# First projections of a cross-attention kernel in another order, and the FFN weights made in later slots

## The reference, cut to what matters

```python
x = x + xattn(layernorm(x), ctx, ctx, mask, w_q, w_k, w_v, w_o)
# xattn: 16 heads of 64; q, k, v projections;
#   softmax(where(mask, -inf, q k^T / 8)) v, heads joined, @ w_o
x = x + ffn(layernorm(x), kernel, bias, a, b)
# ffn: w = quantize_int4(kernel); y = x w + bias + (x a) b
```

## Time and profile before

| what | value |
| --- | --- |
| three executions | 502.39, 502.15, 498.56 us |
| profiled execution: span from first to last instruction | 499.3 us |
| its own time | not given apart from the span |
| mean granted TensorE clock | 0.979 of full speed |
| busy: PE, DVE, ACT, POOL | 451.8, 406.2, 327.6, 398.7 us |
| chain of waits: PE, DVE, ACT, POOL | 43%, 27%, 16%, 8% of the span |
| busy PE, first and second 20 us | 10.76 and 15.70 us |

### The profile page before, as it was taken

The page is one execution under the profiler, slowest core; times in us unless marked ns, Lnnn a source line. Parts: engine busy times, 40 slices in busy tenths (PEclk is TensorE's granted clock), DMA queues, the critical chain, the costliest instruction groups (busy, mean ns, idle before and its releaser), DMA issues.

```text
span 499.3 us, 15466 instructions
## 1 busy us (share of the span) xinstructions
PE 451.8 (90%) x5855; PEld 328.7 (66%) x5855; DVE 406.2 (81%) x1110; ACT 327.6 (66%) x845; POOL 398.7 (80%) x659
## 2 busy tenths in 40 slices
PE   3968989999999999999999999999999999888874
PEld 1434756777766866777766866687667867576662
DVE  4986779987988989788988989898988888778662
ACT  5967566875677766776677766776667666656530
POOL 5687478999788977788788978798797977889931
PEclk9999799999999999999999999999999999899897
DMA  8602685798957996689857985798677877669950
GB/s 284 213 23 43 125 178 113 137 182 169 168 115 144 196 144 118 123 185 161 145 116 141 195 158 119 144 182 160 129 141 128 158 143 142 126 126 177 155 127 27
DMA packets 218817, 71.91 MB, mean 144 GB/s; under 512 B 202785, under 2 KB 216882, under 8 KB 218738
## 3 DMA queue, kind: packets, MB, share of 16 engines
q1 hardware_dynamic: 217680, 69.25, 71.4%
q0 software_dynamic: 480, 1.31, 0.9%
q10 hardware_dynamic: 578, 0.30, 0.2%
HBM read 14.71 MB, written 4.19 MB: 38 GB/s over the span
## 4 chain that ended last, share of the span: by engine, by line
PE 43%; DVE 27%; ACT 16%; POOL 8%; issue 4%; DMA 2%; SPq 0%; DVEq 0%; POOLq 0%; ACTq 0%
PE ps_b L915 32%; ACT arena L673 8%; DVE ps_a L803 7%; PE ps_a L983 6%; DVE arena L796 4%; DVE arena L785 2%; ACT arena L652 2%; DVE arena L871 2%; DMA arena<-in_L_xattn_w_q_dram 2%; POOL arena L580 2%; PE ps_b L1035 2%; POOL arena L584 2%; PE ps_b L1004 2%; ACT arena L664 1%; DVE arena L807 1%
## 5 line engine op out<-in xcount | busy, mean ns | idle before, releaser
L915 PE MATMUL ps_b<-arena 128*128 128x65 f16 (+3 forms) x3348 | 323.6, 249 | 6.1 <-DVE arena L871 3.4
L915 PEld LDWEIGHTS ps_b<-arena 128*128 128x128 f16 x3348 | 224.5, 99 | 81.8 <-issue 6.1
L673 ACT ACTIVATE arena<-ps_a,arena 128x160 f32<-128x160 f32 x512 | 160.0, 396 | 92.6 <-DVE arena L807 84.0
L584 POOL TENSOR_TENSOR arena<-arena 128x512 f16<-128x512 f32 x128 | 148.6, 1161 | 0.0
L580 POOL CAST arena<-arena 128x512 f16<-128x512 f32 x128 | 78.4, 613 | 54.4 <-ACT arena L673 53.1
L803 DVE TENSOR_REDUCE ps_a<-ps_a 128x4 f32<-128x640 f32 x128 | 105.3, 822 | 0.0
L983 PE MATMUL ps_a<-arena 64*128 64x160 f16 x1536 | 76.2, 232 | 13.2 <-ACT arena L673 13.2
L983 PEld LDWEIGHTS ps_a<-arena 64*128 64x128 f16 x1536 | 50.8, 95 | 38.2 <-issue 20.9
L1004 PE MATMUL ps_b<-arena 128*128 128x65 f16 x512 | 72.1, 194 | 0.0
L871 DVE TENSOR_TENSOR arena<-ps_b,arena 128x256 f32<-128x256 f32 x128 | 54.3, 424 | 4.4
L796 DVE TENSOR_TENSOR arena<-ps_b,arena 128x512 f16<-128x512 f32 x60 | 41.1, 686 | 19.1 <-ACT arena L664 17.8
(11 more groups left out here) (139 smaller groups left out, 424.3 us busy)
## 6 DMA issues: line engine op xcount, KB each, us to landing
arena<-in_x_dram SPq DMA_DIRECT2D x8, 512.0 KB, 5.5
mask_u<-in_x_dram SPq DMA_DIRECT2D x32, 128.0 KB, 3.0
out_dram<-mask_u SPq DMA_DIRECT2D x32, 128.0 KB, 2.6
arena<-arena SPq DMA_TRANSPOSE x128, 4.0
arena<-arena SPq DMA_DIRECT2D x24, 65.0 KB, 2.7
arena<-in_L_xattn_w_q_dram SPq DMA_DIRECT2D x1, 1024.0 KB, 8.7
arena<-in_L_xattn_w_k_dram SPq DMA_DIRECT2D x1, 1024.0 KB, 10.7
arena<-in_L_xattn_w_v_dram SPq DMA_DIRECT2D x1, 1024.0 KB, 12.2
```

The source lines that it names most:

```text
L584: nc.gpsimd.tensor_tensor(lo_main, main, hi_main, ALU.subtract)
L673: ins = nc.scalar.activation(probs[k % 2][:, h, :], p_scores[k % 2][:, h % 2, h // 2 * WINDOW:(h // 2 + 1) * WINDOW], ACT.Exp, bias=neg_ma ...
L915: mm = nc.tensor.matmul(dst, a, c, start=(first and at == 0), stop=(last and at == n - 1))
```

## The change

Three things. The first projections get another order: `k0` directly behind `c`, and `r0`, `r1` ahead of `v0`, `v1`; the scores of units 0 to 3 lie behind `q6`, `q7`, `k3` and `v0` (a table, `SCORES_BEHIND`), not behind `k1`, `k2`, `v0` and `r0`. The statistics for the second input lie behind `q7` and `k2`, and POOL's power is taken in slot 0. In the slots of the first batch, the keys of the second batch come in slots 1 and 2, its input's transposes in slot 3, and the queries and values behind them in other slots than before. The FFN pieces move from slots 1, 3, 5 to 6, 8, 10 on DVE, and from 4 to 9 on ACT. For that, the LoRA product gets memory of its own.

```diff
@@ -375,15 +373,17 @@
-        FIRST_PROJ = [["c", "x0"], ["x1"], ["k0", "k1"], ["k2"],
-                      ["k3", "q0"], ["q1"], ["q2"], ["q3", "q4"],
-                      ["q5"], [], ["q6"], ["q7", "v0"],
-                      ["v1"], [], [], []]
+        FIRST_PROJ = [["c"], ["k0", "k1"], ["k2", "k3"], ["x0", "x1"],
+                      ["q0"], ["q1"], ["q2"], ["q3"],
+                      ["q4", "q5"], [], ["q6"], ["q7"],
+                      ["v0"], ["v1"], [], []]
...
-        ALL_PROJ = AHEAD + ["h", "c", "q6", "k0", "q7", "k1", "k2", "k3", "v0", "v1", "r0", "r1"]
+        ALL_PROJ = AHEAD + ["h", "c", "k0", "q6", "k1", "q7", "k2", "k3", "r0", "r1", "v0", "v1"]
+        SCORES_BEHIND = {"q6": 0, "q7": 1, "k3": 2, "v0": 3}
+        NORM_SLOT = 0
@@ -589,11 +594,12 @@
             split_low(nc.gpsimd, 3)
-            norm(2)
 
             def slot(s):
                 if s.k < LAST - 1:
                     split_probs(s.k)
+                if s.k == NORM_SLOT:
+                    norm(2)
@@ -705,11 +711,14 @@
-                if name in ("v1", "r1"):
-                    half = int(name == "r1")
-                    for t in range(ST // 2 * half, ST // 2 * (half + 1)):
+                if name == "r1":
+                    exps(2)
+                if name == "v1":
+                    for t in range(ST // 2):
                         norm_apply(t, 2)
-                    exps(2 + half)
+                    exps(3)
+                    for t in range(ST // 2, ST):
+                        norm_apply(t, 2)
@@ -719,7 +728,7 @@
-                if s.k == 4:
+                if s.k == 9:
                     act.wait_ge(ffn_made, 1)
@@ -810,18 +819,12 @@
-                if name == "k1":
-                    maxima(0)
-                if name == "k2":
-                    maxima(1)
-                if name == "v0":
-                    maxima(2)
-                if name == "r0":
-                    maxima(3)
-                if name == "c":
+                if name in SCORES_BEHIND:
+                    maxima(SCORES_BEHIND[name])
+                if name == "q7":
                     for t in range(ST):
                         norm_stats(t, 32)
-                if name == "k0":
+                if name == "k2":
                     norm_var()
@@ -880,11 +883,11 @@
-                if s.k == 1:
+                if s.k == 6:
                     ffn_grid(dve)
-                if s.k == 3:
+                if s.k == 8:
                     ffn_weights(dve)
-                if s.k == 5:
+                if s.k == 10:
                     dve.wait_ge(split_hi, 5)
...
@@ -1058,6 +1055,8 @@
                 for i, name in enumerate(s.proj):
+                    if s.k < NS and name in ("k0", "q0"):
+                        pe.wait_ge(item_done, first_item("c" if name == "k0" else "x1"))
                     item(s, i, name)
```

## The result

| | us, median (lowest to highest) | ratio to before, 95% interval |
| --- | --- | --- |
| before | 501.79 (498.56 to 502.39, 4 runs) | |
| after | 515.64 (511.94 to 515.9, 4 runs) | 1.0282 [1.0238, 1.0325] |
| forecast | 511.8 (503.5 to 517.5) | |

What follows compares the result with a forecast made beforehand. In slots with a projection, a 3.43 us ACT-DVE round trip sets the pace. Terms 3.5 + 1.4 + 3.2 - 1.1 = 7.0, with the clock's 2.6 9.6, on 502.15 give 511.8 us (chance 0.50); range 503.5 to 517.5.

Steps and rivals of the forecast that it cites:

- A: Program start up to the second batch's k0: scores(2) at 44.5, k0 at 55.8 to 55.9 against 52.41, +3.5 us.
- B: Second batch's k0 to maxima(4): DVE does three keys' low parts first, 4.4 us against 2.97, +1.4 us.
- C: Slots 4 to 15: round-trip loop, q0 behind x1's low part, moved FFN pieces, q5, v1 in slot 13; +3.2 us.
- D: POOL at unit 16: it was behind by about 1.7 us and swallows two thirds of that delay, -1.1 us.
- order, sum: Terms A to D over the first batch and start, without the clock: 3.5 + 1.4 + 3.2 - 1.1 = 7.0 us.
- clock: Half clock behind the 4.7 us wait ahead of the second batch's k0, over three keys and scores: +2.6 us.
- walk: Step-by-step timing from the first projections: scores(2) at 44.5, c's copy at 54.6, second batch's k0 at 55.8 to 55.9.
- rival with both stretches: Rival: the wait ahead of scores(2) also brings half clock, doubling r0, r1, v0, +3.9 us: 515.7; chance 0.14.
- No second stretch: Rival: no second half-clock stretch, so the order's 7.0 us alone: 509.2; chance 0.18.
- given back: Rival: DVE's added work in slots 6 to 15 hides, POOL bounding that batch's end: +2.5 us, 504.7; chance 0.11.
- Faster: Rival: keys run straight behind c, if ACT copies c before 48 us: -5.2 us, 496.9; chance 0.07.
- POOL's root: POOL's normalization root behind the first splitting of probabilities holds the second some 2 us; claimed to cost nothing.

Runs made afterwards that it cites:

- experiment with all waits filled: After, with filler matmuls in four waits of PE (first k0, scores(2), second batch's k0, its q0): 507.14 us, ratio to before 1.012.
- experiments 4: Before, with only the new slot table of the first batch: 507.1 us, ratio 1.0109.
- 7: After, with the old start (first projections, scores 0 to 3, statistics and normalizations as before): 505.33 us, ratio 1.007.
- 10: Before, with 36 filler matmuls in PE's wait ahead of x0 in slot 0: 499.52 us, ratio 0.9975.
- 12: Kernel 11 with filler also at the program's start, 50 matmuls during the mask load and 14 ahead of the first query: 499.89 us, ratio 0.9989.
- experiments 5: Before, with only the FFN pieces moved to slots 6, 8, 10 and 9: 501.45 us, ratio 1.0004.
- 11: The fastest kernel: before with filler ahead of x0 and the FFN grid on DVE moved from slot 1 to slot 0: 498.62 us, ratio 0.995.

## Why the prediction was right, and where not

**The forecast.** Slower, inside the range, by the mechanism named; 3.8 under the median. The experiment with all waits filled takes most of the clock out, so its trace can be set beside the terms of the order. That trace is of an execution of 510.3, and the other four took 506.9 to 508.1, so its sum is rather too high.

| term | forecast | measured |
| --- | --- | --- |
| A: scores(2); `k0` of the second batch | 44.5; 55.8 to 55.9 (+3.5) | 44.66; 56.05 (+3.6) |
| B: `k0` to maxima(4) | 4.4 (+1.4) | 60.25 - 56.05 = 4.20 (+1.2) |
| C: maxima(4) to (16), 40.34 before | +3.2 | 104.20 - 60.25 = 43.95 (+3.6) |
| D: given back by POOL | -1.1 | -0.5 |
| order, sum | 7.0 | 7.9 in the trace; 5.7 by medians (507.14 - 501.44) |
| clock | 2.6 | 8.5 by medians (515.64 - 507.14); 6.1 between the traces |

**A** has the right place for `k0`, in part by luck. The trace began 1.2 earlier than before's (low part of the first `c` at 32.94 for 34.14) and lost about as much in the first stretch. Counted from the end of that low part, scores(2) come 11.3 behind (44.66 - 33.36), where the walk had 9.9 (44.5 - 34.56). From scores(2) to `k0` it took 11.4, and the walk had 11.3 to 11.4: this half, ACT's queue, stands as worked out. **B** stands, by its three low parts. **C** is mainly two small errors: the FFN blocks cost 1.96 (with the waits filled maxima(9) to (10) took 4.31, before 3.44; (11) to (12) 5.37, before 4.28), not 1.6, so less of them is covered; `v1` in slot 13 cost 1.78 for 1.7. **D** was too large: the delay at maxima(16) of 8.48 is 7.96 at maxima(32). The lag of POOL at unit 16 in after fell from 4.03 to 114.95 - 111.48 = 3.47, as said, but by 0.56 only. The prediction took 1.7 as a backlog of which two thirds could swallow delay. In after POOL stands idle 1.17 shortly before, ahead of 111.10, until DVE has finished a variance (L859); there DVE's delay reaches POOL, and no backlog is left. The first cast of unit 16 on POOL:

```profile
114.95 0.62 POOL L585 CAST arena<-arena 128x512 f16<-128x512 f32 x1
```

**The clock is the term that was mis-sized.** The prediction counted one stretch, behind the wait ahead of `k0` at 55.9, and an upper case with the wait ahead of scores(2). The one it took for certain is there (57.8 to 64.5), and its size was about right. Set after's trace beside that with filler, between the same events:

| part | after | waits filled | cost of the clock | forecast |
| --- | --- | --- | --- | --- |
| first `k0` to scores(2) | 12.16 | 11.15 | 1.0 | none |
| scores(2) to the second batch's `k0` | 13.07 | 11.39 | 1.7 | 3.9, as a rival |
| that `k0` to maxima(4) | 6.29 | 4.20 | 2.1 | 2.6 |
| maxima(5) to (6), with `q0` | 5.69 | 4.42 | 1.3 | none |

That is 6.1; the earlier start of the second trace makes up the rest of the 7.28 at maxima(16). So the number of the stretches was wrong, not the price of the one that was counted. The wait ahead of `q0` was in the walk as time only, 0.7 of term C, and no clock was charged for it. In the first row both traces have a stretch, of 6.8 and of 3.4 us, so that the whole of the first one cost more than 1.0. The rival with both stretches, 515.7, has the measured time by luck: its two stretches were priced at 6.5 and cost 3.8. The first stretch is not of the new order alone: the traces of experiments 4, 7, 10 and 12 have the old start and show 3.4 us at half clock that begin between 32 and 34.5, while those of before and of experiments 5 and 11 show none there.

By the Trainium skill, page "TensorE: Matmul & The Clock Gate", section on the HAM clock gate (Part 1), an idle TensorE goes back to half rate and has to work before it is released; the four stretches of after agree. Which waits bring one, the traces without filler at the place show only in part:

| wait ahead of | length, us | followed by half clock |
| --- | --- | --- |
| the second batch's `k0`, or `x0` behind the new start | 3.08 to 4.67 | in 7 of 7 traces |
| `x0` in before and with the FFN pieces alone | 2.23 | in 2 of 2 |
| scores(2), where over 2 us | 2.07 to 2.52 | in 3 of 5, not with the two longest |
| `q0` | 1.40 to 1.57 | in 2 of 6 |

The long wait could be charged for certain, as the prediction did; the shorter ones belonged into the range with a chance each. The trace of before would have shown it. The prediction calls 51.8 to 58.6 the case's one such stretch, but two more, of 3.4 us each, begin there at 434.1 and 468.2, behind waits of 1.62 and 1.68:

```profile
433.60 0.59 PE L983 MATMUL ps_a<-arena 64*128 64x160 f16 x12 [1.62 <-ACT arena L673]
...
468.23 0.98 PE L983 MATMUL ps_a<-arena 64*128 64x160 f16 x12 [1.68 <-ACT arena L673]
```

Other short waits in the same trace, of 1.54 ahead of 26.54 and of 1.12 ahead of 66.17, had full clock behind them.

**The other rivals.** No second stretch (509.2) and given back (504.7) are excluded by the stretches and by the distance of 15.2, of which 15.1 is left at maxima(112) (442.69 against 427.56). Faster (496.9) asked for the copy of `c` on ACT before 48; it came at 58.81. POOL's root, said to cost nothing, costs nothing on the path to exponentials 3: these in after follow the two normalizations ahead of them without a gap (55.74 + 1.08, 56.72).

**Open.** By medians the clock cost 8.5 and the order 5.7, by the traces 6.1 and 7.9; each is one trace, and of the medians one stands on four executions and one on five. Why the wait ahead of `q0` brought a stretch in two traces and none in four stays open. After minus before is 13.6 by the spans and 15.2 at maxima(32); the trace of after lacks the two late stretches of before.

## What to carry to other kernels

When an order is changed, list every wait that it opens on TensorE and charge it twice: its length, and the work behind it at half clock. Here the waits of 3 us and more had to be charged for certain; behind the shorter ones of the table above the half clock came in 7 of 13 cases, so that it belongs into the range. An operation that is ready early is worth nothing while its copy stands behind exponentials and normalizations in another engine's queue; follow the item through every queue before moving it. Where a wait can't be removed, matmuls that nobody reads can cover it (in the first projections and at the program's start here they are not shown to), and they are a test that takes the clock's share apart from the order's.

## What the runs showed that was not expected

- Waits as short as 1.57 and 2.07 us were followed by 3.4 us at half clock, while in other traces waits of 1.57 and 2.52 us at the same places were not.
- The start differs between executions of nearly the same instructions: maxima(0) come at 37.38 in the fastest kernel's trace, 38.80 in before, 40.36 in after. The times of one kernel go with the mean granted clock: of 29 executions of before (experiments 10 to 12), six at 0.986 took 498.0 to 499.3, and three at 0.969 took 503.1 to 503.4; of after, the one at 0.975 took 511.94, those at 0.966 to 0.970 took 515.5 to 515.9. What makes one execution have more half clock than another was not shown, and filler at the start did not change it.
- The clock shown near the start can't be taken at its word. In the trace of before, 18 to 20 us stands at 1.00, but the first queries' six matmuls took 2.74 there, twice the 1.29 of a steady slot; after shows 0.50 at the same place and the same 2.74. PE in before:

```profile
18.06 2.74 PE L1583 MATMUL ps_b<-arena 128*128 128x512 f16 x6 [0.30 <-DVE arena L1514]
```

Where the same matmuls can be compared, their duration is a surer sign of the clock than the record.
